# Regrouping turned softmax blocks pair by pair in an attention and feed-forward kernel

## The reference

```python
xn = _layernorm(x, axis=-1)
# attention
y = layernorm(xn) * ln_w + ln_b
q, k, v = (einsum('bsd,hde->bshe', y, W) + b for W, b in ...)
scores = where(causal, einsum('bqhe,bkhe->bhqk', q, k) * 64 ** -0.5, -inf)
z = einsum('bhqk,bkhe->bqhe', softmax(scores), v)
attn_out = einsum('bqhe,hed->bqd', z, W_o) + b_o
# feed-forward, with W1 and W2 rounded to -1, 0, 1
out = relu(xn @ Wq1.T + b1) @ Wq2.T + b2
x = x + attn_out + out
```

## Time and profile before

| what | value |
|---|---|
| median of 3 runs | 224.38 us (223.8 to 224.81) |
| the profiled execution | 225.33 us, span 223.5 us |
| busy share: PE, PEld, DVE, ACT, POOL | 95%, 84%, 90%, 87%, 83% |
| granted TensorE clock | full throughout |
| DMA traffic | 30.79 MB, 24030 packets |
| regrouping DMAs `pT<-blocks` | 124, 192.0 KB each |

### The profile page before, as it was taken

One profiled execution on the slowest core, in us unless ns is written; L12 is line 12 of the kernel. 1 busy time (PEld: TensorE's weight loads), 2 busy tenths in 40 slices (PEclk: granted clock), 3 DMA queues, 4 the chain that ended last, 5 costly groups with the idle time before them and its releaser, 6 DMA issues.

```text
span 223.5 us, 9672 instructions
## 1 busy us (share of the span) xinstructions
PE 211.9 (95%) x3670; PEld 187.9 (84%) x3670; DVE 201.8 (90%) x776; ACT 195.5 (87%) x733; POOL 184.8 (83%) x363
## 2 busy tenths in 40 slices
PE   7999799999999999999998999989999999999795
PEld 5766498888998899889987999879998998899584
DVE  3499999999999999999999999999999999999931
ACT  0999999997999899997999899997999899996830
POOL 5799989999988989798988899797988985996530
PEclk9999999999999999999999999999999999999999
DMA  5990656606675487636855566636756567677700
GB/s 155 279 273 6 141 116 172 143 3 144 146 158 127 105 196 174 133 78 153 172 134 150 123 147 159 121 84 143 173 119 177 109 152 171 153 165 161 165 5 23
DMA packets 24030, 30.79 MB, mean 138 GB/s; under 512 B 2608, under 2 KB 23088, under 8 KB 23984
## 3 DMA queue, kind: packets, MB, share of 16 engines
q1 hardware_dynamic: 23840, 30.16, 57.5%
q10 hardware_dynamic: 144, 0.02, 0.0%
HBM read 4.73 MB, written 1.05 MB: 26 GB/s over the span
## 4 chain that ended last, share of the span: by engine, by line
PE 46%; ACT 16%; DVE 14%; POOL 11%; DMA 7%; SPq 3%; issue 2%; POOLq 0%; DVEq 0%
PE s_ps L822 8%; DMA pT<-blocks 7%; PE m_ps L862 7%; ACT prob L491 5%; DVE s_ps L603 4%; ACT prob L493 4%; PE m_ps L940 4%; DVE blocks L616 3%; SPq L351 3%; PE m_ps L787 3%; POOL prob L315 3%; ACT qk L480 2%; PE m_ps L789 2%; PE m_ps L788 2%; ACT qk L482 2%; POOL prob L314 2%
## 5 line engine op out<-in xcount | busy, mean ns | idle before, releaser
L491 ACT ACTIVATE prob<-s_ps,neg_max 128x256 f32<-128x256 f32 x128 | 67.6, 528 | 5.6 <-DVE neg_max L603 5.2
L315 POOL TENSOR_SCALAR prob<-prob,inv_sum 128x256 f32<-128x256 f32 x126 | 61.3, 486 | 0.0
L616 DVE STREAM_TRANSPOSE blocks<-prob 128x768 f32<-128x768 f32 x62 | 59.7, 968 | 1.6 <-POOL prob L315 1.6
L314 POOL TENSOR_SCALAR prob<-prob,inv_sum 128x128 f32<-128x128 f32 x126 | 47.5, 377 | 15.4 <-DVE inv_sum L610 15.4
L603 DVE CUSTOM_DVE_ANT_0 s_ps<-s_ps,causal 128x256 f32<-128x256 f32 x128 | 55.1, 430 | 5.0 <-PE s_ps L822 4.5
L493 ACT ACTIVATE prob<-s_ps,neg_max 128x128 f32<-128x128 f32 x128 | 54.0, 422 | 0.0
L862 PE MATMUL m_ps<-pT,v 64*64 64x64 f32 (+2 forms) x1536 | 49.0, 256 | 3.5 <-DMA pT<-blocks 2.1
L822 PE MATMUL s_ps<-qk 64*64 64x128 f32 (+2 forms) x1280 | 49.9, 276 | 0.9 <-ACT prob L493 0.5
L862 PEld LDWEIGHTS m_ps<-pT,v 64*64 64x64 f32 x1536 | 42.5, 133 | 8.8 <-DVE zT_lo L622 3.6
L822 PEld LDWEIGHTS s_ps<-qk 64*64 64x64 f32 x1280 | 42.0, 133 | 7.1 <-issue 3.8
L603 DVE CUSTOM_DVE_ANT_0 s_ps<-s_ps,causal_first 128x128 f32<-128x128 f32 x128 | 42.4, 331 | 0.0
(11 more groups left out here) (120 smaller groups left out, 492.4 us busy)
## 6 DMA issues: line engine op xcount, KB each, us to landing
pT<-blocks SPq DMA_DIRECT2D x124, 192.0 KB, 3.6
xT_cur<-in_xT SPq DMA_DIRECT2D x8, 128.0 KB, 4.2
outT<-out_sb SPq DMA_DIRECT2D x8, 128.0 KB, 4.0
x_all<-in_x SPq DMA_DIRECT2D x1, 768.0 KB, 8.6
wv_raw<-in_w_v SPq DMA_DIRECT2D x2, 256.0 KB, 5.5
wo<-in_w_o SPq DMA_DIRECT2D x1, 512.0 KB, 6.5
x_all<-in_x SPq DMA_DIRECT2D x2, 128.0 KB, 3.9
wq_raw<-in_w_q SPq DMA_DIRECT2D x2, 128.0 KB, 2.5
```

Of the source, the lines that this page charges most:

```text
L314: op(first, first, inv_sum[:, j, 2 + h:3 + h], 0.0, ALU.mult, ALU.add)
L315: last = op(later, later, inv_sum[:, j, h:h + 1], 0.0, ALU.mult, ALU.add)
L491: nc.scalar.activation(later, s_ps[:, pair % 2, h, 0:S].rearrange("p (g j k) -> p g j k", g=TILES, j=QT), ACT.Exp, bias=neg_max[:, j, h:h ...
L616: nc.vector.transpose(blocks[:, duo, :, n, :, :], prob[:, pair % NBUF, :, :, :, :] .rearrange("p h j g k -> p (j g) h k")).then_inc(turned, 1)
```

## The change

A pair now has its own part of `blocks` and of `pT`, its own semaphore `pT_in[pair]`, and its own call of `regroup`, with four DMAs of 768 bytes for each of 128 partitions. The call waits for this pair's turn alone. TensorE waits for both pairs' semaphores ahead of a duo. In SyncE's tables each duo's word becomes its two pairs' words. The other engines' tables stand as they were.

```diff
--- before.py
+++ after.py
@@ -73,9 +73,9 @@
 POOL_HEAD = ("hs np wl2 wl3 ln+ p0 p1 p2 p3 h0 xl+ p4 p5 p6 h1 p7 wl4 wl5 p0+ ln++ p1+ ol p2+ p3+ p4+ xl++ p5+ p6+")
 POOL_PLAN = ("h0- p7- h1- p0 p1 ln+ p2 p3 xl+ p4 p5 p6")
 POOL_TAIL = ("p7- p0 h0- p1 h1- p2 p3 p4 p5 p6 h0 h1")
-SP_HEAD = ("d0 d1 d2 d3 d0+ d1+ d2+ d3+ d0++ st d1++")
-SP_PLAN = ("d2 d3 st- d0+ d1+")
-SP_TAIL = ("d2 st- st")
+SP_HEAD = ("d0 d1 d2 d3 d4 d5 d6 d7 d0+ d1+ d2+ d3+ d4+ d5+ d6+ d7+ d0++ d1++ st d2++ d3++")
+SP_PLAN = ("d4 d5 d6 d7 st- d0+ d1+ d2+ d3+")
+SP_TAIL = ("d4 d5 st- st")
 
 
 def steps(plan, batch):
@@ -184,9 +184,9 @@
 
         prob = sb("prob", [P, NBUF, 2, QT, 3, QB])
 
-        blocks = sb("blocks", [P, DUOS, QT * 3, 2, 2, QB])
-
-        pT = sb("pT", [P, DUOS, QT, 3, 2, 2, QB])
+        blocks = sb("blocks", [P, PAIRS, QT * 3, 2, QB])
+
+        pT = sb("pT", [P, PAIRS, QT, 3, 2, QB])
         neg_max = sb("neg_max", [P, NBUF, 4])
         row_sum = sb("row_sum", [P, NBUF, 4])
         inv_sum = sb("inv_sum", [P, NBUF, 4])
@@ -201,7 +201,7 @@
         wo_in = sem("wo_in")
         w12_in = sem("w12_in")
         vec_in = sem("vec_in")
-        pT_in = [sem(f"pT_in{n}") for n in range(DUOS)]
+        pT_in = [sem(f"pT_in{n}") for n in range(PAIRS)]
         out_done = [sem(f"out_done{n}") for n in range(2)]
 
         xh_first_psd = sem("xh_first_in_psum")
@@ -316,7 +316,7 @@
             return last
 
 
-        pT_last = pT[:, DUOS - 1, :, :, :, :, :].rearrange("p i g n h q -> p (i g n h q)").rearrange("p (n h w) -> p n h w", n=2, h=2)
+        pT_last = pT[:, PAIRS - 2:PAIRS, :, :, :, :].rearrange("p n i g h q -> p n (i g h q)").rearrange("p n (h w) -> p n h w", h=2)
 
         block = ctx.enter_context(nc.Block())
 
@@ -342,15 +342,15 @@
             sp.dma_start(x_all[:, 2 * TILES:NT, :], x_v[:, 2 * TILES:NT, :]).then_inc(x_in[2], 16)
             load_turned(0)
             load_turned(1)
-            def regroup(b, duo):
-
-                wait(sp, turned, PAIRS * b + 2 * duo + 2)
-                wait(sp, z_psd, 4 * (DUOS * (b - 1) + duo + 1))
+            def regroup(b, pair):
+
+                wait(sp, turned, PAIRS * b + pair + 1)
+                wait(sp, z_psd, 4 * (DUOS * (b - 1) + pair // 2 + 1))
                 for i in range(QT):
                     rows = slice(i * QB, i * QB + QB)
-                    sp.dma_start(pT[:, duo, i, :, :, :, :].rearrange("p g n h q -> p (g n h q)"),
-                                 blocks[rows, duo, :, :, :, :].rearrange("k c n h q -> k (c n h q)")
-                                 .rearrange("k (j r) -> k j r", j=QT)).then_inc(pT_in[duo], 16)
+                    sp.dma_start(pT[:, pair, i, :, :, :].rearrange("p g h q -> p (g h q)"),
+                                 blocks[rows, pair, :, :, :].rearrange("k c h q -> k (c h q)")
+                                 .rearrange("k (j r) -> k j r", j=QT)).then_inc(pT_in[pair], 16)
 
             def store(b):
                 wait(sp, o_done, b + 1)
@@ -611,9 +611,8 @@
 
             def turn_blocks(b, pair):
                 wait(dve, prob_ready, PAIRS * b + pair + 1)
-                duo, n = divmod(pair, 2)
-                wait(dve, pT_in[duo], 16 * QT * b)
-                nc.vector.transpose(blocks[:, duo, :, n, :, :], prob[:, pair % NBUF, :, :, :, :]
+                wait(dve, pT_in[pair], 16 * QT * b)
+                nc.vector.transpose(blocks[:, pair, :, :, :], prob[:, pair % NBUF, :, :, :, :]
                                     .rearrange("p h j g k -> p (j g) h k")).then_inc(turned, 1)
 
             def low_heads(b, duo):
@@ -857,7 +856,7 @@
                         if by_tensor:
                             turned_part = pT_last[rows, n, h, tile * P + toks.start:tile * P + toks.stop]
                         else:
-                            turned_part = pT[rows, duo, i, tile + queries.start:tile + queries.stop, n, h, :]\
+                            turned_part = pT[rows, 2 * duo + n, i, tile + queries.start:tile + queries.stop, h, :]\
                                 .rearrange("p i g q -> p g i q")
                         last = nc.tensor.matmul(dst[h * E:h * E + E, n, toks], v[rows, tile, cols], turned_part,
                                                 start=clears, stop=closes)
@@ -871,7 +870,8 @@
                         pe.wait_ge(last_wide, 2)
                         pe.wait_ge(last_narrow, 1)
                     else:
-                        pe.wait_ge(pT_in[duo], 16 * QT * (b + 1))
+                        for pair in (2 * duo, 2 * duo + 1):
+                            pe.wait_ge(pT_in[pair], 16 * QT * (b + 1))
                     product(0, first, 0, both, whole)
                     product(1, later, 0, near, upper)
                     product(1, later, 0, far, whole)
```

## The result

| | before | after |
|---|---|---|
| median of runs | 224.39 us (4 runs, 223.8 to 224.81) | 229.64 us (4 runs: 228.25, 228.53, 230.75, 233.16) |
| profiled execution, its span | 225.33 us, 223.5 us | 228.25 us, 226.5 us |

The change makes the kernel slower: ratio 1.0215, 95% interval 1.0134 to 1.0296. The ratios of this document are of fast executions alone, within 1.5% of their kernel's fastest, which leaves out 233.16 here. The forecast was 226.2 us, with a range from 222.8 to 238. The profiled execution of after is its shortest one; the forecast for it was 227.1 us.

The account below looks back on a forecast made before the run. Steady batches were taken as bound by TensorE, VectorE right behind. Start shifts of +0.55 us and 1.2 us for second waits gave +1.8 us: 227.1 us profiled, 226.2 us median, range 222.8 to 238.

Parts of the forecast that it names:

- its own case: Forecast's main case: p 0.67 to 0.71, kernel at 225 to 228 us, chance 0.42.
- The period p: Time per regrouping issue with its gap on SyncE's queue: 0.69 us taken, bounds 0.64 and 0.78.
- the fourth issue: Last issue of a burst on SyncE's queue: held until the first landing today, just freed by a 2.6 us landing.
- the first rival: SyncE's queue never recovers: fourth issue held as today, p 0.74, kernel at 234 us; chance 0.28.
- the landing: From issue start to landing of a burst's last 96 KB transfer: 2.9 us taken.
- The stalls: Issues over 0.97 us ahead of the fourth, in eight of 31 bursts: some 0.4 us more, average 0.03 per issue.
- a gain of 2.1: Last duos of batches 3 to 5: TensorE's three waits for regrouped blocks go, 2.1 us won.
- the tail: Last products fed by DMA: would start at 214.7 us against 213.44, 1.3 us lost.
- TensorE's second wait: One more semaphore wait per duo, 31 more in all: 0 to 1.6 us, 1.2 us taken.
- The signs named in the forecast: Profile after: median issue near 610 ns, SyncE waiting 20 to 30 us, pT waits at batches 1, 2 and tail only.
- The second rival: Faster: p stays at 0.65, nothing held, second wait hidden under the matmuls, 223.1 us; chance 0.20.
- the third: Rival with nothing to see: gains and losses cancel or the next engine holds the batch, 223.5 to 225.4 us; chance 0.10.

Follow-up runs that it names:

- E10: Changed kernel with one 384 KB copy per pair in place of four DMAs, 62 in all, regrouping left out: 223.77 us, ratio 0.9965.
- E1: Kernel before with each regrouping DMA cut into two of 64 rows of 1536 bytes, 248 issues, start after both turns: 240.38 us, ratio 1.069.
- E3: Changed kernel, but a pair's DMAs wait for both turns of the duo: 240.31 us at full clock, 244.31 to 247.82 in three others.
- E7: Changed kernel with its 248 DMAs as plain copies onto the same 128 partitions, regrouping left out: 230.37 us, ratio 1.0248.
- E9: Changed kernel with each regrouping DMA from batch 1 on moving only 384 bytes of each row: 228.38 us, ratio 1.0193.
- E2: Kernel before with one more TensorE wait per duo, on a count reached long ago: 224.98 us, ratio 0.9997.
- E8: Kernel before for batches 0 and 1, the change's pair transfers from batch 2 on: 229.3 us, ratio 1.020.
- E4: Kernel before with only the last duo of each batch regrouped pair by pair, 20 issues a batch: 224.47 us, ratio 0.9983.

## Why the forecast held, and where it was off

The direction held, and the time lies in the stated range. It lies outside the 225 to 228 us that the forecast gave its own case, by 1.6 us in the median and by 0.3 to 0.5 in the executions at full clock. At full clock the change costs some 4.0 us (228.25 and 228.53 against 224.39) where 1.8 was forecast. That the range held is owed to its width, which came from a rival.

**The mechanism held, as far as it names the issues.** The change was forecast to cost because SyncE's queue can't issue 24 transfers between pair 2's turn and the last duo's products. E10 shows that the early start does what it is for, E1 and E3 that the issues take it back, E7 and E9 that neither pattern nor bytes do.

**The period p: 0.69 taken, 0.71 measured.** (165.9 us of 248 issues make 669 ns, and 0.043 between them.) That the fourth issue is no longer held was right: its 96 KB land in 2.4 us, and undisturbed runs of issues of 0.60 to 0.61 us stand in the chain above. This rules out the first rival's reason, a fourth issue that is still held. Its picture of a queue that is hardly ever free is nearer to the trace than the forecast's, though: 3.2 us of waiting for turns from 72 to 215 us. Where the queue doesn't rest the period is longer than 0.71, as in batch 5 (SyncE's timeline from 148 to 173 us):

```profile
148.94 23.69 SPq L351 DMA_DIRECT2D pT<-blocks  x32
```

That is 0.74 each, and 0.75 in batch 0. By the forecast's own sum each 0.04 above 0.69 is 1.0 us in 24 issues; the landing, 0.5 us shorter than taken, gave half of it back.

**The stalls were mis-sized, and this is the step that failed.** I had read long issues ahead of the fourth as 0.4 us in a quarter of the bursts, 0.03 us per issue, and spread them evenly. Measured against the median they make (165.9 - 248 x 0.604) / 248 = 0.065 us each on average, twice the term, and they aren't spread: 24 of them hold the queue 0.3 to 1.4 us each, 17.8 us in all.

The 0.4 us was a net price that no longer held. In the kernel before, the burst at 65.0 us has an issue of 1579 ns:

```profile
L351 SPq DMA_DIRECT2D pT<-blocks x4: 542/623/1579, 65.0 to 67.9; - x4
```

Its sum is 3.37 us, only 0.4 above the 2.96 of the burst at 114.7 us, because its fourth issue took 642 ns and not 1085. The hold of the fourth, which the forecast read as lasting until the first landing, was then nearly over. With 96 KB the fourth is no longer held, so nothing is saved there and a long issue costs its whole excess, 0.74 us on average. Their number grew too. Both kernels have 29 of the 16 KB packets; of before's, 8 start close to a long issue, of after's 24, as the queue is now issuing nearly all the time.

So batch 0 lost 1.9 us in place of 0.15 (0.36 of it not the queue's), batch 1 lost 1.5 in place of 0.6, and the last duos of batches 3 to 5 kept waits of 1.4 us together, where I had all three gone for a gain of 2.1. From batch 2 to 5 the starts show a gain of only 0.9. Batch 2 gained 0.5 where a loss of 0.6 was forecast, and the tail, behind batch 6, lost 0.5 of 1.3. That a batch which lost time has its turns later too, so that the next has less to catch up, would explain this; it is argued, not shown.

**TensorE's second wait: 1.2 taken, 0 measured** (E2). This error and the landing, 2.4 in place of 2.9, hid part of the stalls' cost: the profiled execution came out at 228.25 us against 227.1. The 0.95 us by which before's profiled execution stood above the median were no constant either: after's profiled one is the shortest of the four.

**What was missing altogether: the clock.** The median is 3.4 us above the forecast, and the profiled execution only 1.15. After's executions at a mean granted clock of 1.0 and 0.998 took 228.53 and 228.25 us, those at 0.993 and 0.978 took 230.75 and 233.16. What such a fall costs is to be seen in E1. First TensorE's timeline at 38 us, then the window view of three stretches (us, busy of PE, PEld, DVE, ACT, POOL, granted clock, DMA share, GB/s):

```profile
38.34 0.92 PE L864 MATMUL m_ps<-pT,v 64*64 64x256 f32 x20 [2.35 <-DMA pT<-blocks]
```

```profile
30.00:38.90 8.90, 6.55 (x136) 6.01 (x134) 8.82 (x39) 8.37 (x33) 8.13 (x15) 1.00 0.76 126
38.90:42.30 3.40, 3.40 (x52) 3.01 (x46) 0.00 (x0) 0.89 (x3) 3.17 (x8) 0.50 0.92 155
42.30:50.00 7.70, 7.65 (x152) 6.57 (x148) 6.85 (x25) 7.64 (x29) 5.30 (x9) 1.00 0.55 97
```

TensorE stood 2.35 us waiting for blocks, was busy 6.55 us of 8.9, and then had 1.2 GHz in place of 2.4 for 3.4 us, in which it did work of 1.7 us at full clock. In E9 the two executions at full clock took 227.49 and 227.70, the two at 0.992 and 0.991 took 229.06 and 229.38, about the same 1.7 us. It can be less: E3's profiled execution has four such stretches and took 4.0 us more than the one without.

The length of the wait ahead of it alone doesn't decide whether the clock falls. In E3's profile it falls in or behind waits of 2.2, 2.4, 2.0 and 1.8 us and not behind one of 2.33; in E7's behind one of 1.43 for the blocks; in E8's behind one of 1.37 at 28.1 us, for v, which stands in the kernel before as well (1.44 us) without a fall. In the profiled execution of after the longest wait is 1.6 us and the clock did not fall before its end. Of the 49 executions of before that stand beside E1 to E10 one had a mean clock of 0.992, the others 0.998 and more, and one each of E2's and E4's twelve had 0.991; two of after's four were at 0.993 and below, and so were four of E1's, three each of E3's and E7's. So the falls are rare without the many issues and frequent with them. That they come by way of TensorE's waits is likely, and no run shows it by itself.

**The signs named in the forecast.** Median issue near 610 ns: 604. Few over 1000: no; 20 were, and 24 over 800. SyncE's wait of 20 to 30 us: 19.6. Waits in batch 1 and the tail: yes; none stands at batch 2. Gone in batches 3 to 5: no. The second rival needed p below 0.66, the third a gain that cancels; neither came.

**What stays open.** That the 16 KB packets hold the issues rests on their coincidence in the traces (24 of 24) alone: in E10 every issue follows a rest, and no run changed the number of packets. What makes the clock fall behind one wait and not behind another is open as well.

## What to carry to other kernels

Before transfers are split for an earlier start, multiply the number of issues by what one costs behind another on that queue and compare it with the time between the data's birth and its use. Then leave room for long issues: where the queue has no rest before the data is used, every one of them counts, not only that of the last burst (batch 0: three, 3.2 us). A price read from a trace in which something else hides a part of it, as the held fourth issue did, must be taken in full when the change removes what hid it. What an earlier start can win here is of the order of the consumer's wait for that data, 2.1 us of 223.5 (E10 won 0.6 us), and a cheap test is a kernel with fewer and larger transfers that start equally early. A new wait of TensorE can cost again as much through the clock: falls stood behind waits of 1.4 to 2.4 us here, though not behind all of them.

## What the hardware showed that I had not expected

- An issue of SyncE's costs about 600 ns behind another, whatever it carries within SBUF: 604 for 96 KB regrouped, 603 for 48 KB, 601 for a plain copy, 595 for rows of 1536 bytes. Only after a rest does the form count: 465 for a plain copy (of 384 KB, too) against 542 ns.
- With the fourth issue of a burst free again, transfers of 96 KB land in 2.4 us from 32 partitions and 2.0 from 128; those of 48 KB in 2.0 too. Half the bytes or a better pattern saves 0.4 us, and four times the bytes in one plain copy cost 0.7 (384 KB, 2.7 us).
- A 16 KB packet of instructions goes with an issue longer by up to 1.4 us when issues stand one behind the other (24 of the 26 that start close to one in after), and with none when each follows a rest (4 in E10).
- A stretch of 3.4 us at the half clock costs up to 1.7 us, and in E1, E3, E7 and E8 each began in or within 2 us behind a wait of TensorE of 1.4 to 2.4 us, so that a kernel's waits can be dearer than their length.
